# A routed expert block: GpSimd's row writes in twos, its stores in threes, an unrolled store loop, and two steps of VectorE sooner

## The chip, the core and the metric

The kernel runs on one core of one Trainium2 chip. Its time is the device time of that core in microseconds. TensorE, VectorE, ScalarE, GpSimd and SyncE (SP) run their own instruction streams and wait for each other by semaphores. A DMA adds 16 to its semaphore when it has landed. In the profile PE is TensorE's products, PEld its weight loads, DVE is VectorE, ACT is ScalarE, POOL is GpSimd.

## The reference, cut to what matters

```python
def reference(x, ctx, g_xattn, g_ffn, Wq, Wk, Wv, Wo, Wg, bg, W1, b1, W2, b2):   # x, ctx: (8, 512, 256)
    def xattn(x, context):                       # 16 heads of 16; attention is over the heads of a token
        Q, K, V = [(a @ W.T).reshape(b, l, 16, 16).swapaxes(-2, -1)
                   for a, W in ((x, Wq), (context, Wk), (context, Wv))]
        attn = softmax(einsum('blih,bljh->blij', Q, K) / 4)
        return einsum('blij,bljh->blih', attn, V).swapaxes(-2, -1).reshape(b, l, 256) @ Wo.T
    def ffn(x):                                  # 8 experts, one per token, width 256
        idx = argmax(softmax(x @ Wg + bg))
        y = einsum('tei,eih->teh', gelu(einsum('th,ehi->tei', x, W1) + b1), W2) + b2
        return y at idx
    x = x + tanh(g_xattn[0]) * xattn(layernorm(x), ctx)
    return x + tanh(g_ffn[0]) * ffn(layernorm(x))
```

## The kernel before, in words

4096 tokens are 32 tiles of 128 rows, taken as 16 pairs of tiles in the attention part (about 0 to 200 us). Two pairs make a batch (8 batches, 0 to 7). For each batch VectorE picks each token's expert (pick_1 to pick_7; pick_7 makes the one-hot `oh_b`), TensorE counts ranks with it (`ranks`, L535 and L537), VectorE makes row numbers (place_1 to place_3), and GpSimd writes the rows of a tile with one indirect DMA to `routed_rows` in DRAM, sorted by expert (`route_tile`, L1411; four writes per batch). Each write adds 16 to the semaphore `routed`. The row that is written carries the mean and the inverse deviation of its token; GpSimd raises the variance to the power -0.5 in `pow_x1` (L1404 and L1406, "the pow step").

The expert part works on 39 blocks of 128 routed rows. Per block b: SP fetches the rows (`fetch`, L391), VectorE normalises them (`norm_b`, L1111), TensorE transposes (L641), ScalarE copies (L800), TensorE runs layer 1 (L651), ScalarE the GELU (L793), TensorE layer 2 (L670), VectorE adds bias and residual (`finish`, L1128 to L1132), and GpSimd writes the 128 rows to `out_rows` with an indirect DMA (`store`, L1467). ScalarE also copies the block's layer 1 weights (L785). TensorE's slot b is layer1(b), layer2(b-1), transpose_b(b+2). ScalarE's is gelu(b), copy_xbt(b+2), copy_w1(b+3). VectorE's is `ahead(b)`, the normalisation of block b+3, and then `behind(b)`, the finish of block b-1. There are 8 buffers for finished rows, each with a semaphore `stored[j]`, j = b % 8; VectorE's finish of b waits for the store of b-8.

Blocks 0 to 15 may start before the last rows are written. So the part overlaps with the end of attention and with batches 6 and 7, whose picking, ranks and row numbers are spread over the first slots by hand. SP fetches block 16 and on when the table of blocks is made (`tab_done`) and all 32 writes have landed.

For the last three blocks (36, 37, 38) VectorE computes bias and residual ahead in `prepare` (L1146), and `finish_ahead` (L1157) adds only the product, for block 38 in two halves. YL_ORDER lists in what order the three are prepared.

GpSimd's program is in order: the loop over pairs, `end()`, then stores 0 to 15 written out with the last batch's four writes behind store 3, then a loop with 8 stores per turn (blocks 16 to 31), then blocks 32 to 38 written out. In all of them a store with an odd number is followed by a wait for the landing of the store before it, except from block 36 on. In the loop and before block 16 a wait goes through `wait_apart`, which takes a further instruction.

The helpers `wait_apart` and `slots` stay as they are.

## Time and profile before

| | us |
|---|---|
| median of 3 runs | 291.73 (291.23 to 291.84) |
| the profiled execution | 290.77 |
| its span in the profile | 288.9 |
| TensorE's products busy | 275.6 |
| VectorE busy | 211.3 |
| GpSimd busy | 130.4 |
| ScalarE busy | 102.9 |

The span runs from the first to the last instruction; 1.9 us of the profiled execution lie around it. The granted clock of TensorE is full throughout. In a timeline a row gives an instruction's start, its length, and in brackets how long its engine was idle before it and what the profile names as the end of that idle time. An indirect DMA's row shows the time in which GpSimd issues it, not its landing.

### The profile page before, as it was taken

The page shows a single profiled execution, that of the slowest core. Times are in us where ns is not written, and L with a number is a line of the kernel's source. Part 1 is how long each engine was busy: PE and PEld are TensorE (multiplying, and loading weights), DVE is VectorE, ACT ScalarE, POOL GpSimd, SP SyncE. Part 2 cuts the span into 40 slices and gives each one's busy share as a digit, 9 for nine tenths or more (in the row PEclk, how much of TensorE's full clock was granted, in tenths as well). Part 3 has the DMA queues.
Part 4 walks back from the last instruction along what each step waited for, and adds up shares of the span by engine and source line. Part 5 has one row for each costly group of instructions (what it writes and reads, how often), then busy time and mean ns, then how long its engine had stood idle before and what let it go on. Part 6 is the DMA issues. An engine that isn't in the chain of part 4 may idle for free.

```text
span 288.9 us, 9745 instructions
## 1 busy us (share of the span) xinstructions
PE 275.6 (95%) x3185; PEld 219.2 (76%) x3186; DVE 211.3 (73%) x613; ACT 102.9 (36%) x258; POOL 130.4 (45%) x156
## 2 busy tenths in 40 slices
PE   8999999999999999999999999799987999999990
PEld 7667777677776776777767777578976988998980
DVE  7667667787796786878778778788876875765661
ACT  2120311302203113031130321337664776776750
POOL 9623032243524525336254452702754554455565
PEclk9999999999999999999999999999999999999999
DMA  7955355476664755647656634414244344433311
GB/s 233 297 163 161 71 138 146 127 205 171 192 178 144 224 175 182 208 122 225 170 174 226 193 103 135 126 42 117 84 149 133 112 151 143 121 113 124 97 71 40
DMA packets 31242, 43.24 MB, mean 150 GB/s; under 512 B 7662, under 2 KB 18543, under 8 KB 31217
## 3 DMA queue, kind: packets, MB, share of 16 engines
q1 hardware_dynamic: 17760, 21.35, 26.7%
q10 hardware_dynamic: 10048, 12.99, 15.1%
q0 software_dynamic: 3408, 8.59, 8.4%
q8 instruction: 12, 0.20, 0.3%
q14 instruction: 14, 0.11, 0.2%
HBM read 24.83 MB, written 10.60 MB: 123 GB/s over the span
## 4 chain that ended last, share of the span: by engine, by line
PE 75%; issue 7%; POOL 5%; DVE 5%; DMA 5%; ACTq 1%; ACT 1%; POOLq 0%; DVEq 0%
PE ps_qo L439 18%; PE ps_pr L410 18%; PE ps_av L484 11%; PE ps_so L465 9%; POOL out_rows L1467 5%; PE ps_av L670 3%; PE ps_so L651 3%; PE ps_to L670 3%; PE ps_tr L474 3%; PE ps_tr L651 3%; PE ps_to L497 2%; PE ps_pr L641 2%; DMA sb_kb<-sb_y_k 2%; DMA out_rows<-sb_q_n,sb_tok_i 2%; DVE sb_kb L1279 1%
## 5 line engine op out<-in xcount | busy, mean ns | idle before, releaser
L410 PE MATMUL ps_pr<-sb_wkv,sb_ct 128*128 128x512 f32 x120 | 57.7, 605 | 0.0
L718 ACT ACTIVATE sb_pe_x<-sb_pe_x 128x512 f32<-128x512 f32 x16 | 10.1, 631 | 111.9 <-DVE sb_pe_x L894 100.6
L1397 POOL TENSOR_SCALAR sb_ve<-sb_mv 128x2 f32<-128x2 f32 x16 | 3.5, 220 | 78.0 <-DVE sb_mv L853 75.2
L1411 POOL DMA_INDIRECT routed_rows<-sb_xs,sb_pos_i x32 | 32.7, 1023 | 12.5 <-issue 7.4
L410 PEld LDWEIGHTS ps_pr<-sb_wkv,sb_ct 128*128 128x128 f32 x120 | 20.5, 190 | 17.7 <-issue 17.3
L484 PE MATMUL ps_av<-sb_vb,sb_at 128*32 128x128 f32 x1024 | 31.8, 274 | 1.5 <-issue 1.5
L465 PE MATMUL ps_so<-sb_kb,sb_y_q 128*32 128x128 f32 x1024 | 31.2, 273 | 0.5 <-DMA sb_kb<-sb_y_k 0.5
L484 PEld LDWEIGHTS ps_av<-sb_vb,sb_at 128*32 128x32 f32 x1024 | 27.2, 110 | 5.1 <-issue 4.9
L439 PE MATMUL ps_qo<-sb_wog,sb_ot 128*128 128x264 f32 x120 | 29.6, 388 | 0.0
L439 PEld LDWEIGHTS ps_qo<-sb_wog,sb_ot 128*128 128x128 f32 x120 | 22.5, 190 | 9.2 <-issue 6.4
L465 PEld LDWEIGHTS ps_so<-sb_kb,sb_y_q 128*32 128x32 f32 x1024 | 28.0, 110 | 1.9 <-issue 1.5
L439 PE MATMUL ps_qo<-sb_wqg_c,sb_xt 128*128 128x264 f32 x120 | 29.3, 387 | 0.0
L879 DVE STREAM_TRANSPOSE sb_y_q<-sb_q_n 128x512 f32<-128x512 f32 x16 | 17.4, 1090 | 15.6 <-ACT sb_q_n L713 15.5
L785 ACT COPY sb_kb<-sb_w_all 128x514 f32 x39 | 24.2, 622 | 11.0 <-issue 10.4
L303 POOL TENSOR_TENSOR sb_cn<-sb_om,sb_rt 128x512 f32<-128x512 f32 x14 | 18.1, 1290 | 20.3 <-DVE sb_om L918 20.3
L1467 POOL DMA_INDIRECT out_rows<-sb_y_k,sb_tok_i x20 | 20.0, 1001 | 15.8 <-issue 9.8
L439 PEld LDWEIGHTS ps_qo<-sb_wqg_c,sb_xt 128*128 128x128 f32 x120 | 21.7, 190 | 3.8 <-issue 0.5
L670 PE MATMUL ps_av<-sb_w,sb_ht 128*128 x80 | 20.6, 380 | 1.1 <-issue 0.6
L651 PE MATMUL ps_tr<-sb_ct,sb_kb 128*128 128x128 f32 x152 | 20.3, 276 | 1.3 <-ACT sb_ct L800 1.3
L651 PE MATMUL ps_so<-sb_ct,sb_kb 128*128 128x128 f32 x160 | 21.2, 276 | 0.2 <-ACT sb_ct L800 0.2
L670 PE MATMUL ps_to<-sb_w,sb_ht 128*128 x76 | 20.0, 385 | 0.3 <-ACT sb_ht L793 0.2
L651 PEld LDWEIGHTS ps_so<-sb_ct,sb_kb 128*128 128x128 f32 x160 | 19.5, 192 | 0.5 <-ACT sb_ct L800 0.5
(159 smaller groups left out, 493.0 us busy)
## 6 DMA issues: line engine op xcount, KB each, us to landing
sb_x<-x_in ACTq DMA_DIRECT2D x16, 256.0 KB, 3.5
sb_kb<-sb_y_k SPq DMA_DIRECT2D x124, 32.0 KB
sb_vb<-sb_y_v SPq DMA_DIRECT2D x120, 32.0 KB
sb_ct<-ctx_in ACTq DMA_DIRECT2D x14, 256.0 KB, 3.1
sb_xt<-xt_in_ ACTq DMA_DIRECT2D x14, 256.0 KB, 4.6
sb_xb<-routed_rows SPq DMA_DIRECT2D x25, 134.0 KB
sb_w_all<-w_in_ SPq DMA_DIRECT2D x4, 514.0 KB
sb_w<-w_in SPq DMA_DIRECT2D x4, 512.0 KB
```

Of the source, the lines that this page charges most:

```text
L303: eng.tensor_tensor(cn[:].rearrange("p u h i -> p h u i"), om[:].rearrange("p h (u i) -> p h u i", u=2), rt[:].rearrange("p (u i) -> p u i ...
L410: last = pe.matmul(pr[:, s * 512:(s + 1) * 512], lhsT=ct[i][:, kc, s, :], rhs=wkv[:, :, kc, :], start=(kc == 0), stop=(kc == KC - 1))
L439: last = pe.matmul(dst[:, s * 512:s * 512 + DE], lhsT=src[:, kc, s, :], rhs=w[:, kc, :], start=(kc == 0), stop=(kc == KC - 1))
L465: last = pe.matmul(so[32 * q:32 * q + 32, r * P:(r + 1) * P], lhsT=y_q[:, 4 * q + r, u:u + 2, :].rearrange("p a b -> p (a b)"), rhs=kb[i][ ...
L484: last = pe.matmul(av[32 * q:32 * q + 32, r * P:(r + 1) * P], lhsT=at[:, 4 * r + q, u:u + 2, :].rearrange("p a b -> p (a b)"), rhs=vb[i][: ...
L651: last = pe.matmul(h_ps[i][:, ic * P:(ic + 1) * P], lhsT=w1_sb[q % W1_RING][:, kc * D + ic * P:kc * D + (ic + 1) * P], rhs=xbt[i][:, kc, : ...
L670: last = pe.matmul(dst, lhsT=ht[i][:, ic, :], rhs=w2_sb[:, bass.ds(ex, 1), ic, first:end].rearrange("p a d -> p (a d)"), start=(ic == 0), ...
L718: act.activation(pe_x[:], pe_x[:], ACT.Exp, scale=float(H) ** -0.5).then_inc(exp_done, 1)
L785: act.copy(w1_sb[q % W1_RING], w1_all[:, bass.ds(ex, 1), :].rearrange("p a f -> p (a f)")).then_inc(w1_done, 1)
L879: dve.transpose(y_q[:, :, 0:3:2, :].rearrange("p a u i -> p i u a"), q_n[:].rearrange("p s (h i) -> p i s h", h=H)).then_inc(yq_out, 1)
L1411: pool.indirect_dma_start(rows, bass.IndirectOffsetOnAxis(ap=row_numbers(batch)[:, c:c + 1], axis=0), rows_of(j)[:, s, :], None).then_inc( ...
L1467: pool.indirect_dma_start(out, bass.IndirectOffsetOnAxis(ap=tok_i[j][:, 0:1], axis=0), yf[j], None, bounds_check=limit, oob_is_err=False). ...
```

## The change

- Batch 5's four writes in `end()`: the pow step of pair 12 goes between the first two and the last two.
- Batch 6: the pow step of pair 15 goes between its first and second write; a wait for the first write's landing goes ahead of the third, and one for the third's landing behind the fourth.
- The second and fourth write of batches 6 and 7 signal a new semaphore, `routed_odd`, and SP waits for both semaphores before block 16.
- Batch 7, behind store 3: a wait for store 2's landing is put ahead of the writes; the wait behind the second write is for the first write alone, that behind the fourth for the third alone. Before, they were for all so far.
- Stores: from block 4 on they go in threes (4, 5, 6, then 7, 8, 9, and so on). Behind the third GpSimd waits for the landing of the second, up to block 33.
- The loop for blocks 16 to 31 is unrolled; its waits are plain ones.
- VectorE's `pick_7` of the last batch goes ahead of the normalisation of block 7, and `prepare(38)` goes from slot 36 to slot 35.

```diff
-YL_ORDER = (0, 2, 1)
+YL_ORDER = (2, 0, 1)
@@ SP
-            sp.wait_ge(routed, 32 * pairs)
+            sp.wait_ge(routed, 32 * pairs - 64)
+            sp.wait_ge(routed_odd, 64)
@@ VectorE
-                if known and b == blocks - AHEAD:
+                if known and b == blocks - AHEAD - 1:
                     prepare(blocks - 1)
@@
             behind(3, 3, 0)
+            pick_7(m)
             ahead(4, 4, 0)
-            pick_7(m)
@@ GpSimd
-                route_tile(2 * (batch % 2) + i // 2, i % 2, batch)
+                route_tile(2 * (batch % 2) + i // 2, i % 2, batch, routed_odd if i % 2 else routed)
+
+            def late_routed(batch, i):
+
+                return 64 * (last_batch - 1) + 32 * (batch - last_batch + 1) + 16 * (i // 2 + 1)
@@ end()
-                for j in range(2):
-                    route(2 * ((m - 1) % 2) + j, m - 1)
+                route(2 * ((m - 1) % 2), m - 1)
                 pow_x1(n - 2, (n - 2) % 4)
+                route(2 * ((m - 1) % 2) + 1, m - 1)
                 pow_x1(n - 1, (n - 1) % 4)
                 pow_x1(n, n % 4)
-                for i in range(2):
-                    route_nth(m, i)
+                route_nth(m, 0)
                 pow_x1(n + 1, (n + 1) % 4)
-                for i in range(2, 4):
-                    route_nth(m, i)
+                route_nth(m, 1)
+                pool.wait_ge(routed, late_routed(m, 1))
+                route_nth(m, 2)
+                route_nth(m, 3)
+                pool.wait_ge(routed, late_routed(m, 3))
@@ the stores
                 store(b, b % RING, b // RING)
                 if b == 3:
+                    pool.wait_ge(stored[2], 16)
                     for i in range(4):
                         route_nth(last_batch, i)
                         if i % 2 == 1:
-                            pool.wait_ge(routed, 32 * pairs - 16 * (3 - i))
-                elif b % 2 == 1:
+                            pool.wait_ge(routed, late_routed(last_batch, i))
+                elif b == 1 or b > 3 and b % 3 == 0:
                     pool.wait_ge(stored[(b - 1) % OUT], 16 * ((b - 1) // OUT + 1))
-            def store_in_twos(b, q, turn):
-                store(b, q, turn)
-                if isinstance(b, int) and b >= blocks - 3:
-                    return
-                if q % 2 == 1 and isinstance(b, int):
-                    pool.wait_ge(stored[q - 1], 16 * (turn + 1))
-                elif q % 2 == 1:
-                    wait_apart(pool, stored[q - 1], 16 * (turn + 1), passed_pool)
-
-            block_slots(pool, store_in_twos, 0)
+            for b in range(EARLY, blocks):
+                store(b, b % RING, b // RING)
+                if b % 3 == 0 and b < blocks - 3:
+                    pool.wait_ge(stored[(b - 1) % OUT], 16 * ((b - 1) // OUT + 1))
```

Line numbers of the changed kernel are 2 higher in TensorE's and VectorE's part and 8 higher for the store.

GpSimd in `end()`, before: `sb_xs_1` and `sb_xs_0` are the two batches' row buffers, `sb_ve1` the pow step's variance.

```order
L1411 DMA routed_rows<-sb_xs_1,sb_pos_i 33792x268 [waits pos_done]
L1411 DMA routed_rows<-sb_xs_1,sb_pos_i 33792x268
L1411 DMA routed_rows<-sb_xs_1,sb_pos_i 33792x268 [waits pos_done]
L1411 DMA routed_rows<-sb_xs_1,sb_pos_i 33792x268
L1404 TENSOR_SCALAR sb_ve1<-sb_xs_0 128x2 [waits res_pow,res_step]
L1406 TENSOR_TENSOR sb_xs_0<-sb_ve1,sb_neg_half 128x2 [waits res_var]
```

The same place in the changed kernel:

```order
L1413 DMA routed_rows<-sb_xs_1,sb_pos_i 33792x268 [waits pos_done]
L1413 DMA routed_rows<-sb_xs_1,sb_pos_i 33792x268
L1406 TENSOR_SCALAR sb_ve1<-sb_xs_0 128x2 [waits res_pow,res_step]
L1408 TENSOR_TENSOR sb_xs_0<-sb_ve1,sb_neg_half 128x2 [waits res_var]
L1413 DMA routed_rows<-sb_xs_1,sb_pos_i 33792x268 [waits pos_done]
L1413 DMA routed_rows<-sb_xs_1,sb_pos_i 33792x268
```

The pow step now parts the four writes into two pairs.

GpSimd from batch 7's first write on, behind store 3, in the changed kernel; `tok_i_j` is the row list of the store that signals `stored[j]`:

```order
L1475 DMA out_rows<-sb_q_n,sb_tok_i_3 4096x256 [waits yf_done]
L1413 DMA routed_rows<-sb_xs_1,sb_pos_i 33792x268 [waits stored2,pos_done]
L1413 DMA routed_rows<-sb_xs_1,sb_pos_i 33792x268
L1413 DMA routed_rows<-sb_xs_1,sb_pos_i 33792x268 [waits routed]
L1413 DMA routed_rows<-sb_xs_1,sb_pos_i 33792x268
L1475 DMA out_rows<-sb_y_k_1,sb_tok_i_4 4096x256 [waits routed,yf_done]
L1475 DMA out_rows<-sb_y_k_1,sb_tok_i_5 4096x256 [waits yf_done]
L1475 DMA out_rows<-sb_y_v_0,sb_tok_i_6 4096x256 [waits yf_done]
L1475 DMA out_rows<-sb_y_v_0,sb_tok_i_7 4096x256 [waits stored5,yf_done]
```

Before, the first write has no wait for `stored2`, and the wait for `stored4` stands ahead of store 6; here store 6 follows store 5 at once, and store 7 waits for `stored5`.

VectorE around the last batch's one-hot, before: `sb_ct` is the normalised block, `sb_lw` the picked expert's code.

```order
L976 TENSOR_REDUCE sb_lw<-sb_le 128x4 [waits pick_step]
L1128 ISA [waits y_done]
L1128 TENSOR_TENSOR sb_yo<-ps_av,sb_b 128x256
L1130 TENSOR_TENSOR sb_tok_i<-sb_xb,sb_skip 128x1
L1132 SCALAR_TENSOR_TENSOR sb_q_n<-sb_yo,sb_tg,sb_xb 128x256 [waits yb_done]
L1111 TENSOR_SCALAR sb_ct<-sb_wkv 128x256 [waits xbt_done,xb_in7]
L982 TENSOR_TENSOR sb_oh_b<-sb_le,sb_lw 128x32 [waits rank_done,pick_step]
```

And in the changed kernel:

```order
L1134 SCALAR_TENSOR_TENSOR sb_q_n<-sb_yo,sb_tg,sb_xb 128x256 [waits yb_done]
L984 TENSOR_TENSOR sb_oh_b<-sb_le,sb_lw 128x32 [waits rank_done,pick_step]
L1113 TENSOR_SCALAR sb_ct<-sb_wkv 128x256 [waits xbt_done,xb_in7]
L1130 ISA [waits y_done]
L1130 TENSOR_TENSOR sb_yo<-ps_to,sb_b 128x256
```

The one-hot changes places with the normalisation of block 7.

## Rows read from the trace of the kernel before

**Rows 1.** The page: busy us, share and instructions; shares of the chain.

```profile
PE 275.6 (95%) x3185; PEld 219.2 (76%) x3186; DVE 211.3 (73%) x613; ACT 102.9 (36%) x258; POOL 130.4 (45%) x156
PE 75%; issue 7%; POOL 5%; DVE 5%; DMA 5%; ACTq 1%; ACT 1%; POOLq 0%; DVEq 0%
```

**Rows 2.** Table by stretch: us, busy us per engine, granted clock, DMA share, GB/s.

```profile
222.00:282.00 60.00, 59.66 (x415) 54.20 (x414) 39.84 (x130) 42.22 (x116) 31.72 (x32) 1.00 0.39 119
```

**Rows 3.** Timeline at batch 5's writes: start, us, instruction, idle time before and releaser.

```profile
181.40 1.09 POOL L1411 DMA_INDIRECT routed_rows<-sb_xs,sb_pos_i  x1 [0.17 <-issue]
...
186.31 0.32 POOL L1404 TENSOR_SCALAR sb_ve<-sb_xs 128x2 f32<-128x2 f32 x1
...
187.54 1.04 PE L484 MATMUL ps_av<-sb_vb,sb_at 128*32 128x128 f32 x28 [1.15 <-issue]
...
188.80 0.72 DVE L918 STREAM_TRANSPOSE sb_om<-ps_av 128x512 f32<-128x512 f32 x1 [1.97 <-PE ps_av L484]
```

**Rows 4.** Timeline at the last batch's one-hot and ranks, 206 to 213 us.

```profile
206.44 0.19 DVE L953 TENSOR_TENSOR sb_lg<-sb_xs 128x32 f32<-128x32 f32 x1 [0.92 <-POOL sb_xs L1406]
...
210.29 0.18 PE L535 MATMUL ps_qo<-sb_oh_b,sb_tri 128*128 128x40 bf16 x1 [0.36 <-DVE sb_oh_b L982]
...
210.54 0.99 POOL L1467 DMA_INDIRECT out_rows<-sb_y_k,sb_tok_i  x1 [0.30 <-issue]
...
210.91 0.37 ACT L800 COPY sb_ct<-ps_pr 128x256 f32<-128x256 f32 x1 [2.09 <-remote]
...
211.17 1.13 PE L670 MATMUL ps_av<-sb_w,sb_ht 128*128 x4 [0.61 <-issue]
...
212.55 0.63 ACT L793 ACTIVATE sb_ht<-ps_tr,sb_kb 128x128 f32<-128x128 f32 x2
```

**Rows 5.** Timeline at the run of stores 2, 3 and batch 7's writes.

```profile
217.57 0.96 POOL L1411 DMA_INDIRECT routed_rows<-sb_xs,sb_pos_i  x1 [0.30 <-issue]
...
219.54 0.37 ACT L800 COPY sb_ct<-ps_pr 128x256 f32<-128x256 f32 x1 [2.97 <-PE ps_pr L641]
...
219.96 1.16 PE L651 MATMUL ps_tr<-sb_ct,sb_kb 128*128 128x128 f32 x8 [1.34 <-ACT sb_ct L800]
...
221.54 1.13 PE L670 MATMUL ps_av<-sb_w,sb_ht 128*128 x4 [0.42 <-ACT sb_ht L793]
```

**Rows 6.** Timeline: block 4 finished, stores 4 and 32, layer 1 starts of four blocks.

```profile
214.34 0.48 DVE L1132 SCALAR_TENSOR_TENSOR sb_y_k<-sb_yo,sb_tg,sb_xb 128x256 f32<-128x256 f32 x1
...
225.05 0.99 POOL L1467 DMA_INDIRECT out_rows<-sb_y_k,sb_tok_i  x1 [2.41 <-DVE sb_y_k L1132]
...
226.68 1.06 PE L651 MATMUL ps_so<-sb_ct,sb_kb 128*128 128x128 f32 x8
...
257.31 1.06 PE L651 MATMUL ps_tr<-sb_ct,sb_kb 128*128 128x128 f32 x8
...
259.29 1.06 PE L651 MATMUL ps_so<-sb_ct,sb_kb 128*128 128x128 f32 x8
...
278.33 0.98 POOL L1467 DMA_INDIRECT out_rows<-sb_y_k,sb_tok_i  x1 [1.08 <-issue]
...
279.42 1.05 PE L651 MATMUL ps_so<-sb_ct,sb_kb 128*128 128x128 f32 x8
```

**Rows 7.** Timeline of the tail, 280 us to the end.

```profile
280.51 0.48 DVE L1157 SCALAR_TENSOR_TENSOR sb_y_k<-ps_av,sb_tg,sb_yo 128x256 f32<-128x256 f32 x1
...
281.02 0.98 POOL L1467 DMA_INDIRECT out_rows<-sb_q_n,sb_tok_i  x1 [0.42 <-DMA out_rows<-sb_y_k,sb_tok_i]
...
281.82 0.61 PE L670 MATMUL ps_tr<-sb_w,sb_ht 128*128 x4
...
283.49 0.48 DVE L1157 SCALAR_TENSOR_TENSOR sb_y_k<-ps_to,sb_tg,sb_yo 128x256 f32<-128x256 f32 x1 [1.93 <-issue]
...
285.62 0.35 DVE L1157 SCALAR_TENSOR_TENSOR sb_y_v<-ps_tr,sb_tg,sb_y_q 128x128 f32<-128x128 f32 x1 [1.03 <-remote]
...
286.27 0.98 POOL L1467 DMA_INDIRECT out_rows<-sb_y_v,sb_tok_i  x1 [0.31 <-issue]
```

More of the change, by code:

```diff
@@ L251, in flamingo_block @@
         routed = sem("routed")
+        routed_odd = sem("routed_odd")
         pad_in = sem("pad_in")
@@ L1406, in pow_x1, with route_tile @@
                 pool.tensor_tensor(rows_of(j)[:, :, RSTD], ve1[:], neg_half[:], ALU.pow).then_inc(res_pow, 1)
-            def route_tile(j, s, batch):
+            def route_tile(j, s, batch, done):
                 c = 2 * (j % 2) + s
                 pool.indirect_dma_start(rows, bass.IndirectOffsetOnAxis(ap=row_numbers(batch)[:, c:c + 1], axis=0),
-                                        rows_of(j)[:, s, :], None).then_inc(routed, 16)
+                                        rows_of(j)[:, s, :], None).then_inc(done, 16)
             def route(j, batch):
@@ L1417, in route @@
                 for s in range(2):
-                    route_tile(j, s, batch)
+                    route_tile(j, s, batch, routed)
             def route_nth(batch, i):
```

## The prediction

> **What bounds the kernel now.** I read the busy line and the shares of the chain first, then the stretch of the expert blocks, then each engine's timeline where the change sits. TensorE is busy for 275.6 of 288.9 us and holds 75% of the chain; GpSimd holds 5% [rows 1]. TensorE's last product, of block 38, is over at 281.82 + 0.61 = 282.43 us [rows 7]. So TensorE bounds the kernel up to there, and the stores do after it. Gaps of TensorE stand in few places: 1.15 us at 187.54 [rows 3], 0.36 and 0.61 at 210.29 and 211.17 [rows 4], 1.34 and 0.42 at 219.96 and 221.54 [rows 5]. From 222 to 282 it is busy for 59.66 of 60 us [rows 2].
>
> The tail: VectorE adds the bias of block 37 at 283.49 and of the last half of block 38 at 285.62, 3.2 us after the product; the last store starts at 286.27 [rows 7]. GpSimd is behind all the way to there. It stores block 4 at 225.05, though its rows were finished at 214.34 + 0.48 = 214.82, and block 32 at 278.33 [rows 6]: 28 blocks in 53.28 us, 1.90 each or 3.81 a pair. TensorE needs (279.42 - 226.68) / 26 = 2.03 us a block [rows 6], so GpSimd catches up by 0.13 us a block, too little for its ten.
>
> The gaps: where GpSimd issues indirect DMAs back to back (0.96 to 1.0 us each, 0.30 between), the end of TensorE's work reaches the other engines late. In the run of four that ends at 217.57 + 0.96 = 218.53, ScalarE's copy at 219.54 had stood 2.97 us for a transpose, and TensorE then stood 1.76 us in two pieces [rows 5]. In the run that ends at 210.54 + 0.99 = 211.53, ScalarE's copy stood 2.09 us and its next GELU began at 212.55 [rows 4]. I call this the **hold**; both times it is over 1.0 us behind the last issue. Pairs with a wait between them hardly show it: an undisturbed slot is 259.29 - 257.31 = 1.98 us [rows 6], so the 26 slots lost 26 x 0.05 = 1.3 us, 0.1 per pair. A run of four cost 1.76.
>
> **The change part by part.** The profiled execution took 290.77 us (span 288.9 and 1.9 around it); the median of the runs is 291.73. I make the sum against the former; it moves the median by as much.
>
> (a) Batch 5's writes, behind the loop's exit. Now four stand in a row from 181.40 to 186.3, and TensorE stands 1.15 us in the middle of one group of products [rows 3]. The pow step goes between the second and the third. Its operands are there: now it starts at 186.31 with no idle time [rows 3]. It takes about 1.1 us, so the second pair is over at 187.4, and nobody waits for its writes before the fetches. VectorE's transpose of those products, at 188.80, carries the chain on. If the gap goes wholly it gains 1.15; if it has another cause, 0. With a hold of 0.6 to 1.0 behind 187.4 the transpose starts 0.4 to 0.8 sooner. I take **-0.6**.
>
> (b) Batch 6's writes and the one-hot. The pow step moves ahead of the second write and ends about a microsecond sooner, so VectorE's 0.92 us of waiting for it at 206.44 goes [rows 4]. The one-hot then also goes ahead of a normalisation (0.4 us). It is ready at about 208.8, not 210.1, and TensorE's 0.36 for it and 0.61 behind it [rows 4] are covered by layer 1 of block 5. The writes now form a run of three, over at about 209.1, instead of a run of two writes and two stores over at 211.53, so ScalarE's copy comes at about 209.7. What is late next is ScalarE's GELU, still 1.64 us behind that copy. Bounds: -0.3 (the one-hot gains alone and the hold stays) and -1.3 (VectorE's whole gain). I take **-0.9**, near the two gaps of 0.97 that go.
>
> (c) Stores 2, 3 and the last batch's writes. Now stores 2, 3 and writes 0, 1 are the run of 1.76 us. Afterwards the wait for store 2's landing parts the stores from the writes. But between the writes the wait is now for the first of two: for both it was 2.41 us ahead of store 4 [rows 6], for the first of a pair it is 0.42 where the loop is unrolled [rows 7]. A run of four is made again, of the four writes. I take **0**; bounds -1.76 (0.4 us is enough of a break) and +0.3. Behind the new waits stand the stores, 10 us late anyway, and SP's fetch of block 16 onward, which asks for all writes. The shorter waits give back what the added one takes, so the fetch stays hidden, as it is now [rows 2].
>
> (d) Stores in threes. Up to block 15 a run takes 3.81 + 1.28 = 5.09 us, 1.70 a block. From 16 on, unrolled, a pair takes 281.02 - 278.33 = 2.69 [rows 6, 7], as the last ones do now, and three take 3.97. GpSimd starts block 4 some 2 us sooner and TensorE's blocks come 1.5 us sooner: it is 9.7 us behind. It gains 6.1 + stalls - 5.1, some 1.9 us per three, up to block 15, and 3 per three after: level with VectorE at about block 19. From there each store waits for its own block, they stand 2 us apart, and no run is left. The price is four runs of three, back to back, beside working TensorE. No such run is in the trace. Its bounds are 0.1 (a pair) and 1.76 (four); I take the middle, 0.93, since a three has one issue more than the one and one less than the other: 4 x 0.93 = **+3.7**. The pairs' **-1.3** goes. Bounds of both together: -0.9 and +7.5 (five runs at 1.76).
>
> (e) Tail. The bias step of block 38 moves to a place where VectorE waits for TensorE's product anyway. With GpSimd level, block 36 is done at 280.51 + 0.48 and stored at 281.3, 37 at 282.6, 38 at 283.9, against 286.27 [rows 7]: **-2.4**. If the moved step lets 36 come 0.6 sooner, -3.0; if VectorE's last steps stay late, -0.3.
>
> Sum: -0.6 - 0.9 + 0 + 3.7 - 1.3 - 2.4 = **-1.5**: 289.3 profiled, **290.2 us** as a median.
>
> **The rivals.** *A: threes cost no more than twos.* For: pairs cost next to nothing, and TensorE's ends pass in the first half of a run. Against: the stands of 2.09 and 2.97 us. Then (d) is 4 x 0.1 - 1.3 = -0.9, and the time is 291.73 - 0.6 - 0.9 - 0.9 - 2.4 = 286.9 us. The Trainium skill (DMA: Bandwidth & Descriptors, Anatomy of one DMA) says that many descriptors can be emitted before their cost shows; by that sentence this rival is right, while the trace shows a cost on other engines, at 219.54 and 219.96 [rows 5].
>
> *B, slower: a run of three costs what four cost.* The place is blocks 4 to 18, the price 1.76 for each of five runs, 8.8 - 1.3 = +7.5, and the time 291.73 - 0.6 - 0.9 + 7.5 - 2.4 = 295.3 us. The change is slower from where a run costs more than (0.6 + 0.9 + 1.3 + 2.4) / 4 = 1.3 us. For: the hold lasts 1.0 us beyond the last issue, so a three's is 1.28 us longer than a pair's, and a slot of 1.98 us has room for only a part of that. Against: only a product that ends early in the hold pays in full.
>
> *C: the change doesn't do what it says.* GpSimd's runs move, but the last three stores are issued back to back as now and VectorE's last steps stay late: (e) is -0.3; and (a) is 0, since the gap at 187 is no hold. 291.73 - 0.9 + 2.4 - 0.3 = 292.9 us.
>
> **How the numbers follow.** Forecast 0.42, its own range 288.6 to 291.9 (a three at 0.6 to 1.3); A 0.28; B 0.16; C 0.14. Within 0.2% is about what a measurement of this kernel can tell from no change: 291.15 to 292.31. Of the forecast 0.33 lies below 291.15; with A that makes faster 0.61. Within: 0.07 of the forecast, 0.05 of C, 0.02 of B, 0.14 in all. Slower: 0.25. The range goes down to A's 286.9, less half a microsecond for (c), 286.4, and up to 293.4, which leaves out the dearer part of B.
>
> **What the profile of the changed kernel would show.** (a) A pow step between two pairs of writes, and no gap of TensorE inside L484's group. (b) The rank product without idle time before it, and no wait of VectorE for GpSimd's pow. (c) Stores 2 and 3 apart from the writes, the four writes close together, and ScalarE's copy standing near them. (d) Three stores 1.28 us apart up to about block 15, from 19 on one each 2 us; some 3.5 us of gaps in TensorE's blocks, all before block 18. (e) The last store's start 1.5 us behind TensorE's end instead of 3.8. It is wrong if TensorE shows no gaps beside the threes (A), if more than 1.3 us stand beside each (B), or if the last store starts over 3 us behind TensorE's end (C).

## The result, and the profile of the changed kernel

The changed kernel is slower. Its median is 294.12 us (291.48 to 297.82, 22 executions) against 291.75 (290.61 to 293.58, 22 executions) for the kernel before, run beside it; the ratio is 1.006, 95% interval 1.0037 to 1.0083. The forecast was 290.2 with a range of 286.4 to 293.4: the time is above the range. (The medians here take every execution; the ratios leave out those more than 1.5% above the fastest of the same kernel, five of the changed kernel's 22, so they show less than the medians where the times spread.) The executions of the changed kernel also lie further apart (6.3 us from end to end, against 3.0), and the one that was profiled is the lowest of them, 291.48 (span 289.6; before 290.77 and 288.9). So the first reading below shows a mild case. A second profile, near the median, stands with the experiments.

The page of the changed kernel, busy time and chain, answers to [rows 1]. TensorE is busy for 3.1 us more than before and holds 91% of the chain; GpSimd, which held 5%, is off it:

```profile
PE 278.7 (96%) x3185; PEld 221.6 (77%) x3186; DVE 210.3 (73%) x613; ACT 103.3 (36%) x258; POOL 129.4 (45%) x156
PE 91%; DVE 3%; issue 2%; ACT 1%; ACTq 1%; POOL 0%; DVEq 0%
```

More busy time for the same products means a lower clock or stretched groups. The table by stretch (us, TensorE's busy time, that of its weight loads, VectorE's, ScalarE's and GpSimd's, then the granted clock, DMA share, GB/s) shows where. [Rows 2] had 59.66 of 60 us at 1.00:

```profile
220.00:230.00 10.00, 8.21 (x44) 7.07 (x43) 5.32 (x21) 4.82 (x14) 5.80 (x7) 0.83 0.36 111
230.00:285.00 55.00, 52.61 (x364) 47.55 (x362) 33.95 (x107) 37.34 (x101) 28.78 (x30) 1.00 0.38 116
```

A mean of 0.83 over 10 us, of two levels (2.4 and 1.2 GHz), is 3.4 us at the lower one, in which 1.7 us of work is lost, since TensorE was busy throughout it. TensorE's timeline has the places (start, us, instruction, in brackets the idle time before and what ended it):

```profile
187.73 0.38 PE L486 MATMUL ps_av<-sb_vb,sb_at 128*32 128x128 f32 x3 [0.32 <-issue]
188.47 0.53 PE L486 MATMUL ps_av<-sb_vb,sb_at 128*32 128x128 f32 x10 [0.36 <-issue]
...
211.13 1.13 PE L672 MATMUL ps_av<-sb_w,sb_ht 128*128 x4 [0.74 <-ACT sb_ht L795]
...
223.67 1.16 PE L653 MATMUL ps_tr<-sb_ct,sb_kb 128*128 128x128 f32 x8 [1.30 <-issue]
225.32 1.76 PE L672 MATMUL ps_av<-sb_w,sb_ht 128*128 x4 [0.49 <-ACT sb_ht L795]
...
235.96 1.13 PE L672 MATMUL ps_av<-sb_w,sb_ht 128*128 x4 [0.49 <-issue]
...
240.65 1.13 PE L672 MATMUL ps_av<-sb_w,sb_ht 128*128 x4 [0.42 <-issue]
...
285.08 0.71 PE L672 MATMUL ps_av<-sb_w,sb_ht 128*128 x4 [1.32 <-ACT sb_ht L795]
285.62 0.61 PE L672 MATMUL ps_tr<-sb_w,sb_ht 128*128 x4
```

Against [rows 3 to 5]: the gap of 1.15 us at 187.54 is down to two small pieces, and the 0.36 for the ranks is gone. The gap of 1.34 and 0.42 is there still, now 1.30 and 0.49, and behind its second piece the same four products take 1.76 us instead of 1.13: the clock had fallen. Two gaps of 0.4 to 0.5 us and one of 1.32 at block 38 are new. TensorE ends at 286.23, 3.8 us later than in [rows 7]. GpSimd's timeline and ScalarE's copy beside it:

```profile
218.11 0.99 POOL L1413 DMA_INDIRECT routed_rows<-sb_xs,sb_pos_i  x1 [1.00 <-issue]
219.40 0.96 POOL L1413 DMA_INDIRECT routed_rows<-sb_xs,sb_pos_i  x1 [0.30 <-issue]
221.00 0.95 POOL L1413 DMA_INDIRECT routed_rows<-sb_xs,sb_pos_i  x1 [0.64 <-DMA routed_rows<-sb_xs,sb_pos_i]
222.26 0.96 POOL L1413 DMA_INDIRECT routed_rows<-sb_xs,sb_pos_i  x1 [0.30 <-issue]
223.24 0.37 ACT L802 COPY sb_ct<-ps_pr 128x256 f32<-128x256 f32 x1 [2.86 <-PE ps_pr L643]
224.46 0.99 POOL L1475 DMA_INDIRECT out_rows<-sb_y_k,sb_tok_i  x1 [1.25 <-issue]
...
286.90 0.98 POOL L1475 DMA_INDIRECT out_rows<-sb_y_v,sb_tok_i  x1 [0.71 <-DVE sb_y_v L1159]
```

The four writes of the last batch are the new run: ScalarE's copy stands 2.86 us beside it, as it stood 2.97 in [rows 5]. The last store starts 0.67 us behind TensorE's end instead of 3.84. So the end was mended more than forecast, and TensorE lost more than that before it.

### The profile page after: what moved, and what is told of

It is laid out like the page before. It is cut to its first block, busy times and chain, and to the rows that moved or that the text cites. A ratio compares the mean times of both kernels' runs of the same rounds, so it can differ in the third digit from the quotient of the medians.

```text
span 289.6 us, 9704 instructions
## 1 busy us (share of the span) xinstructions
PE 278.7 (96%) x3185; PEld 221.6 (77%) x3186; DVE 210.3 (73%) x613; ACT 103.3 (36%) x258; POOL 129.4 (45%) x156
## 4 chain that ended last, share of the span: by engine, by line
PE 91%; DVE 3%; issue 2%; ACT 1%; ACTq 1%; POOL 0%; DVEq 0%
PE ps_pr L412 19%; PE ps_qo L441 18%; PE ps_av L486 10%; PE ps_so L467 8%; PE ps_so L653 7%; PE ps_av L672 7%; PE ps_tr L653 5%; PE ps_to L672 5%; PE ps_pr L643 4%; PE ps_tr L476 3%; PE ps_to L499 2%; PE ps_av L580 1%; PE ps_pr L426 1%; PE ps_to L433 1%; ACTq L785 1%
## 5 line engine op out<-in xcount | busy, mean ns | idle before, releaser
L672 PE MATMUL ps_av<-sb_w,sb_ht 128*128 x80 | 21.5, 392 | 3.7 <-ACT sb_ht L795 2.7
L653 PE MATMUL ps_so<-sb_ct,sb_kb 128*128 128x128 f32 x160 | 22.1, 283 | 0.2 <-ACT sb_ct L802 0.2
L653 PEld LDWEIGHTS ps_so<-sb_ct,sb_kb 128*128 128x128 f32 x160 | 20.4, 199 | 0.5 <-ACT sb_ct L802 0.5
L653 PEld LDWEIGHTS ps_tr<-sb_ct,sb_kb 128*128 128x128 f32 x152 | 18.5, 191 | 1.8 <-issue 1.5
```

Of the source, the lines that this page charges most:

```text
L653: last = pe.matmul(h_ps[i][:, ic * P:(ic + 1) * P], lhsT=w1_sb[q % W1_RING][:, kc * D + ic * P:kc * D + (ic + 1) * P], rhs=xbt[i][:, kc, : ...
L672: last = pe.matmul(dst, lhsT=ht[i][:, ic, :], rhs=w2_sb[:, bass.ds(ex, 1), ic, first:end].rearrange("p a d -> p (a d)"), start=(ic == 0), ...
```

## The experiments

Kernels that are told of together ran on one chip, against executions of the kernel before among them. "Before" is its median there. I call GpSimd's standing time between two groups of issues its **pause**.

| run | median | before | ratio of the times, 95% |
|---|---|---|---|
| changed kernel, stores in twos (e1) | 295.37 | 292.35 | 1.0093, 1.0059 to 1.0126 |
| before, threes, unrolled (e2) | 294.68 | 292.35 | 1.0078, 1.0051 to 1.0105 |
| before, twos, unrolled (e3) | 296.23 | 292.35 | 1.0117, 1.008 to 1.0154 |
| before, writes and one-hot (e4) | 291.59 | 292.35 | 0.9979, 0.9952 to 1.0006 |
| changed kernel again (a1) | 293.39 | 291.53 | 1.0012, 0.9971 to 1.0053 |
| e3 again (a2) | 294.81 | 291.53 | 1.0094, 1.0055 to 1.0133 |
| e3, idle pow from block 16 (g5) | 292.63 | 291.53 | 1.0018, 0.9981 to 1.0055 |
| e1, idle pow from block 16 (g6) | 292.66 | 291.53 | 1.0024, 0.9985 to 1.0064 |
| changed kernel, idle pow (h1) | 292.76 | 292.34 | 1.0022, 0.9994 to 1.005 |
| before, singles, two idle additions (h2) | 295.53 | 292.34 | 1.013, 1.0085 to 1.0174 |
| e3, half the rows (h5) | 292.83 | 292.34 | 1.0012, 0.9985 to 1.0039 |
| changed kernel, store loop of before (e6) | 291.91 | 292.34 | 0.9985, 0.9954 to 1.0016 |
| e4 and one idle pow (k1) | 291.84 | 292.16 | 0.9985, 0.9955 to 1.0016 |
| e4 again (k2) | 291.53 | 292.16 | 0.9998, 0.9962 to 1.0035 |

Four more runs (g1 to g4) fell on a chip that behaves otherwise; they stand further below.

### Is it the threes, the writes or the unrolled loop?

e1 puts the twos back into the changed kernel, e2 and e3 change the store loop of the kernel before alone, e4 keeps the writes and the one-hot alone.

```diff
 e1: changed kernel, and the same before block 16    e3: kernel before, loop unrolled, this condition
-                if b % 3 == 0 and b < blocks - 3:
+                if b % 2 == 1 and b < blocks - 3:
 e2: kernel before, the changed kernel's unrolled loop of threes
 e4: changed kernel without it
-            for b in range(EARLY, blocks):
-                ...
+            block_slots(pool, store_in_twos, 0)            (and twos before block 16)
-YL_ORDER = (2, 0, 1)         (and prepare(blocks - 1) back behind block 36)
+YL_ORDER = (0, 2, 1)
```

> The changed kernel with its stores in twos again from block 4 on (loop unrolled; the writes, one-hot and tail edits kept). Theory T, the threes cost (about 0.9 us each beside working TensorE, one of them with a drop of the granted clock to half behind it): the time falls from 294.1 by 3.5 or more, to 288.5 to 290.5 us, and no gap over 0.6 us stands in TensorE's blocks from 222 to 245. Theory W, the four writes of the last batch, parted only by short waits, cost and start it: the time stays at 293.5 to 294.5 and a gap of 1 us or more still stands near 222. Theory U, the unrolled loop costs (GpSimd's stores move onto other work): 293 or more, with gaps that are spread over the blocks.

> The kernel before with its stores in threes and unrolled, nothing else changed. Theory T: slower than before by 2 to 4 us less the gain at the end of 1 to 2 us: 293 to 295 us. Theory W (the writes cost, the threes don't): 290 to 291.5 us. Theory U: 293 to 295 us as well, and the kernel with unrolled twos tells it from T.

> The kernel before with the store loop unrolled and still in twos, nothing else changed. Theory T: GpSimd catches up by 1.1 us a pair from block 16 on, the last store starts 1.5 us behind TensorE's end instead of 3.8: 289.0 to 290.5 us. Theory U: 292.5 us or more. Theory W says the same as T here.

> The kernel before with the edits of the writes and the sooner one-hot alone (batch 5 and 6 split by the pow steps, the waits for the first of two, stores 2 and 3 parted from the last batch's writes); stores in twos in the loop and the tail as before. Theory T: the prediction's terms for them, -1.5 us: 290.2 (289.5 to 291.5). Theory W: the last batch's four writes in a row cost 1.8 us or more and set the clock back: 292.5 to 294 us, with a gap of TensorE of over 1 us near 222.

Theory T, mine, isn't enough. Without any three the changed kernel is no faster (295.37), and the kernel before with nothing but its loop unrolled is 3.9 us slower: the worst of the four. In threes the unrolled loop costs 2.3. The writes and the one-hot alone do no harm (-0.8, the interval just holds zero), so W falls. What e3 shows is U: something that unrolling brings, with a place, behind block 16. But e1 doesn't refute T. It took the threes out and got another thing for them: its profile's large gaps stand beside the pairs of blocks 16 to 20, 1.34 us an issue,

```profile
250.18 1.16 PE L653 MATMUL ps_tr<-sb_ct,sb_kb 128*128 128x128 f32 x8 [1.92 <-issue]
...
254.96 2.07 PE L672 MATMUL ps_av<-sb_w,sb_ht 128*128 x4 [3.62 <-ACT sb_ht L795]
```

where the changed kernel, whose GpSimd is level with VectorE from store 17 or 18 on, has none. In the repeated run of unrolled twos (a2) TensorE's timeline reads

```profile
250.35 1.16 PE L651 MATMUL ps_tr<-sb_ct,sb_kb 128*128 128x128 f32 x8 [0.77 <-issue]
...
255.75 2.07 PE L670 MATMUL ps_av<-sb_w,sb_ht 128*128 x4 [4.24 <-ACT sb_ht L793]
```

and the table by stretch, of TensorE alone,

```profile
250.00:260.00 10.00, 5.41 (x24) 0.66 0.20 58
```

Some 5 us of standing still in the middle of the blocks, and then half clock (2.07 us for products that take 1.13). GpSimd and ScalarE beside it:

```profile
246.19 1.17 POOL L1467 DMA_INDIRECT out_rows<-sb_y_v,sb_tok_i  x1 [0.30 <-issue]
247.70 0.98 POOL L1467 DMA_INDIRECT out_rows<-sb_y_k,sb_tok_i  x1 [0.34 <-issue]
...
250.38 0.98 POOL L1467 DMA_INDIRECT out_rows<-sb_q_n,sb_tok_i  x1 [0.42 <-DMA out_rows<-sb_y_k,sb_tok_i]
251.67 0.98 POOL L1467 DMA_INDIRECT out_rows<-sb_q_n,sb_tok_i  x1 [0.30 <-issue]
253.13 0.98 POOL L1467 DMA_INDIRECT out_rows<-sb_y_k,sb_tok_i  x1 [0.48 <-DMA out_rows<-sb_q_n,sb_tok_i]
...
254.98 0.62 ACT L793 ACTIVATE sb_ht<-ps_so,sb_kb 128x128 f32<-128x128 f32 x2 [3.64 <-remote]
```

From 244.87 to 254.11 GpSimd issues seven stores with pauses of 0.34 to 0.48 us. ScalarE's GELU starts at 254.98, 0.87 us behind the last of them, though the products that it needs, of the block before, were over at 248.51. The bracket names no instruction, only an event that came late. This is the hold of the prediction, in a run of pairs that I had taken to be parted. In the five profiles with the loop its pauses are 0.95 us or more; unrolled they are 0.34 to 0.48 here. The loop as such need not be the reason: the pairs before block 16 are written out in both kernels, and their pauses are 0.89 us or more too. There, as in the loop, the store's wait for its rows goes through `wait_apart`; from block 16 of the unrolled code, and in the last stores of [rows 7], it is a plain one. No run parts the two.

### Does a pause end it?

g5 and g6 put one small pow of GpSimd on an idle tile behind each wait from block 16 on; a1 and a2 are the changed kernel and e3 once more, on the same chip.

```diff
                 if b % 2 == 1 and b < blocks - 3:
                     pool.wait_ge(stored[(b - 1) % OUT], 16 * ((b - 1) // OUT + 1))
+                    pool.tensor_tensor(idle[:], ve[:], neg_half[:], ALU.pow).then_inc(idled, 1)
```

> The changed kernel once more, beside the others on one chip. The last four runs showed no gap of TensorE beside runs of four and six of GpSimd's issues, nor the gap inside the products at 187 us, in code that was as in the kernel before there; the hold may be a thing of the chip that a run falls on. Theory C (it is): where the kernel before shows its gaps at 187 and 220 us on this chip, this one is 1.5 to 2.5 us slower than before (293.5 to 295); where the hold is absent, it is 2 us or more faster than before. Theory P alone (only pauses decide, on every chip): 1.5 to 2.5 us slower on any chip.

> The kernel before with the store loop unrolled and in twos, once more. Theory C: with the hold on this chip 3 to 4 us slower than before, with gaps of 3 us and more in sum between 245 and 262; without it 1 to 2 us faster than before and no gap there. Theory P alone: 3 to 4 us slower on any chip.

> As the run before this one, with GpSimd's idle pow (0.9 us with what lies around it) behind each wait from block 16 on. Theory P, on a chip that shows the hold: its pairs now stand 1.3 us apart instead of 0.42 and the gaps between 245 and 262 us are gone: 3 us or more faster than the unrolled twos without the pow, 290.5 to 292.5. If pauses don't matter but the run's length in issues over a longer stretch does: gaps of 1 us and more remain, and it is within 1.5 us of the unrolled twos.

> The changed kernel with its stores in twos, unrolled, and the idle pow behind each wait from block 16 on; writes, one-hot and tail edits kept. Theory P, on a chip that shows the hold: 289 to 291.5 us, faster than the changed kernel by 2 us or more and than the kernel before by 0.5 or more, with the gaps near 223 (1.4 us in sum) as the only ones over 0.5 after 215. The rival: TensorE has gaps of a microsecond and more beside the pairs after 245, and it is no faster than the changed kernel.

With the pow the 5 us at 250 are gone. g5's only gap of TensorE from 223 to its end, and GpSimd there:

```profile
248.57 1.13 PE L672 MATMUL ps_av<-sb_w,sb_ht 128*128 x4 [0.38 <-ACT sb_ht L795]
...
249.61 0.72 POOL L1466 TENSOR_TENSOR sb_idle<-sb_ve,sb_neg_half 128x2 f32<-128x2 f32 x1 [0.23 <-DMA out_rows<-sb_y_k,sb_tok_i]
250.52 1.04 POOL L1475 DMA_INDIRECT out_rows<-sb_q_n,sb_tok_i  x1 [0.19 <-POOL sb_idle L1466]
```

So work that does nothing gave 2.2 us back (292.63 against 294.81; by the ratios, whose intervals only just touch, the same). The pause is the cause, or what it stands for. g6 wasn't faster than the kernel before, though I had expected that: with the pow a pair takes 3.5 to 4.3 us, GpSimd doesn't catch up, and its last store starts at 286.52, as late as in [rows 7].

a1 is the case near the median (293.37 in its profile). TensorE, and VectorE at the first gap:

```profile
231.21 0.53 DVE L1113 TENSOR_SCALAR sb_ct<-sb_xb 128x256 f32<-128x256 f32 x1 [3.96 <-DMA sb_xb<-routed_rows]
231.79 0.44 PE L643 MATMUL ps_pr<-sb_cst,sb_ct 128*128 128x128 f32 x2 [1.68 <-issue]
...
239.73 1.12 PE L672 MATMUL ps_to<-sb_w,sb_ht 128*128 x4 [0.39 <-issue]
241.71 1.16 PE L653 MATMUL ps_tr<-sb_ct,sb_kb 128*128 128x128 f32 x8 [0.64 <-issue]
246.42 2.07 PE L672 MATMUL ps_av<-sb_w,sb_ht 128*128 x4 [3.55 <-ACT sb_ht L795]
```

Two things come together. The first gap isn't a hold: VectorE stands for the fetch of a block's rows. The last batch's writes now wait for store 2's landing (1.40 us here) and for the first write's (1.34), the last of them starts at 223.98, and SP asks for block 16 at 229.55, against 227.89 in the kernel before. In e6, further below, the same fetch starts at 231.02 and TensorE stands for 1.99 us. The others are the hold: GpSimd issued four threes (blocks 4 to 15) from 226.02 to 243.45, with pauses of 0.99, 1.15 and 0.99 us, and a further store 0.80 later; the 3.55 and the half clock stand behind the last of them:

```profile
246.00:250.00 4.00, 3.58 (x13) 0.57 0.30 82
```

These are threes before the unrolled part, so in the changed kernel itself it is a chain of threes that costs. In the mild execution the same threes had pauses of 1.39, 1.14 and 1.45. So a few tenths of a microsecond of landing time seem to decide whether a delay adds up and whether a fetch comes late, and that would spread the changed kernel's times; it is argued from two profiles. By the median a1 is 1.9 us slower than before, while its ratio, 1.0012, can't be told from 1.

### The pause, the rate, the threes, or the rows?

h1 is the changed kernel with the pow behind all its waits; h2 has no wait for a landing, but two idle additions behind each single store; h5 is e3 with the stores of the first 64 rows.

```diff
 h1: changed kernel
                 if b % 3 == 0 and b < blocks - 3:
                     pool.wait_ge(stored[(b - 1) % OUT], 16 * ((b - 1) // OUT + 1))
+                    rest()
 h2: kernel before, unrolled (rest is two additions here)
-                if b % 2 == 1 and b < blocks - 3:
-                    pool.wait_ge(stored[(b - 1) % OUT], 16 * ((b - 1) // OUT + 1))
+                if b < blocks - 3:
+                    rest()
 h5: kernel before, unrolled
-                ... IndirectOffsetOnAxis(ap=tok_i[j][:, 0:1], axis=0), yf[j], ...
+                ... IndirectOffsetOnAxis(ap=tok_i[j][0:P // 2, 0:1], axis=0), yf[j][0:P // 2], ...
```

> The changed kernel with GpSimd's idle pow (0.9 us) behind each of its waits between the threes, so that a three is followed by a pause of about 2 us instead of 1.0 and goes at some 1.8 us a block instead of 1.5. The prediction's term (each run of three costs 0.9 us by itself): four gaps of TensorE of about 0.9 us remain, and more threes, so it is slower than the changed kernel or equal. Theory R (what costs is the mean rate of issues over several runs: below some 1.6 us an issue the delay adds up from run to run): no gap over 0.4 us between 226 and 280 us, no half clock there, and 1.5 us or more faster than the changed kernel, unless VectorE comes to wait for stores.

> The kernel before, its store loop unrolled, no wait for a landing at all behind a store; instead two small idle additions of GpSimd (0.22 us each) behind each store, so that single stores stand about 0.75 us apart, 1.75 a block. Theory P (only a pause of about a microsecond lets the delay go): the delay adds up from store to store as in the unrolled twos, gaps of 3 us and more in sum, 294 us or more. Theory R (the mean rate decides): no gap over 0.4 us after 226, 290 to 292 us, and the last store less than 3 us behind TensorE's end.

> The unrolled twos with stores of the first 64 rows of a block only (the other rows of the output aren't written). If the delay comes with each row's descriptor of an indirect DMA: with half of them the gaps that the unrolled twos show between 245 and 262 (3 to 5 us and the half clock) go, 290 to 292 us. If it comes with each issue, whatever its size, or with GpSimd's being level: gaps as in the unrolled twos, 294 or more.

h1 has five threes; the wait in front of the pow grew shorter by as much as the pow took, so the pauses are 0.97 to 1.94 us and not the 2 that I had meant. TensorE, and GpSimd at the last of the gaps:

```profile
237.09 1.13 PE L674 MATMUL ps_to<-sb_w,sb_ht 128*128 x4 [1.16 <-DVE sb_yo L1132]
...
241.90 1.13 PE L674 MATMUL ps_to<-sb_w,sb_ht 128*128 x4 [0.60 <-ACT sb_ht L797]
...
246.84 1.13 PE L674 MATMUL ps_to<-sb_w,sb_ht 128*128 x4 [0.73 <-ACT sb_ht L797]
...
251.42 1.13 PE L674 MATMUL ps_to<-sb_w,sb_ht 128*128 x4 [0.37 <-ACT sb_ht L797]
...
251.68 1.04 POOL L1483 DMA_INDIRECT out_rows<-sb_q_n,sb_tok_i  x1 [0.19 <-issue]
253.03 0.99 POOL L1483 DMA_INDIRECT out_rows<-sb_y_k,sb_tok_i  x1 [0.30 <-issue]
...
255.32 1.13 PE L674 MATMUL ps_av<-sb_w,sb_ht 128*128 x4 [1.66 <-ACT sb_ht L797]
```

The first three (blocks 4 to 6) has no gap behind it, the other four have 1.16, 0.60, 0.73 and 0.37: (0 + 1.16 + 0.60 + 0.73 + 0.37) / 5 = 0.57 on average. The 1.66 stands behind two issues only, stores 19 and 20, 0.97 us after a three: not the price of a three, but what had added up by then. The 1.16 and the 0.37 belong to threes behind pauses of 1.94 and 1.75 us. Theory R, which said no gap over 0.4, is wrong on this: a three that stands alone can cost, somewhat less than the prediction's 0.93. But none grows to 3 us and the clock stays at 1.00. By the median h1 is 0.4 us from its kernel before, where a1 was 1.9; by the ratios (1.0022 and 1.0012) the two are alike, so that the pow made this kernel faster isn't shown.

h2 has single stores with 0.72 us between them, mostly 1.74 from start to start, from 251 on:

```profile
271.65 1.02 POOL L1476 DMA_INDIRECT out_rows<-sb_q_n,sb_tok_i  x1 [0.15 <-issue]
273.39 1.02 POOL L1476 DMA_INDIRECT out_rows<-sb_y_k,sb_tok_i  x1 [0.15 <-issue]
...
280.73 0.71 PE L672 MATMUL ps_av<-sb_w,sb_ht 128*128 x4 [1.88 <-DVE sb_y_k L1159]
```

and TensorE's table by stretch has

```profile
222.00:278.00 56.00, 55.53 (x392) 1.00 0.39 116
```

There is no gap but one of 0.49 at 222.47. Theory P (only a pause of a microsecond helps) is wrong: 0.72 will do, behind each store. The time is bad all the same, 295.53: until 250 the idle steps and their waits took 2.1 us a block, GpSimd fell behind TensorE, VectorE stood for a store's landing (the 1.88 at 280.73) and the last store began 8 us behind TensorE's end. I had forecast 290 to 292 there and missed that.

h5 halves the rows of each issue. An issue takes 0.91 us instead of 0.98, and the gaps at 250 are gone, but so is the cause as stated: from 228 on the landings left pauses of 0.95 to 1.02 us, and GpSimd was level by 246. In that stretch of pairs, 3.2 us each, TensorE still has

```profile
232.43 1.13 PE L670 MATMUL ps_av<-sb_w,sb_ht 128*128 x4 [0.32 <-ACT sb_ht L793]
...
235.17 1.13 PE L670 MATMUL ps_to<-sb_w,sb_ht 128*128 x4 [0.50 <-issue]
...
238.29 1.12 PE L670 MATMUL ps_av<-sb_w,sb_ht 128*128 x4 [0.77 <-issue]
```

Small gaps that grow, at half the rows. And at 218.22, behind two such stores and two whole writes in a row, TensorE stood 2.35 us, against 1.34 + 0.42 in [rows 5]. This speaks for the issue and against the rows as what counts, but it doesn't settle it.

Taken together, by the mean distance of issues over several of them: 1.90 us (loop of before) and 1.79 (h2 from 251.87 on): no gap. 1.63 to 1.8 (g5, 237 to 250): one of 0.38. 1.6 (h5): 0.32, 0.50, 0.77. 1.53 to 1.79, in threes (h1): 0.4 to 1.7. 1.56 to 1.67, in threes (the changed kernel's mild profile): 0.42 and 0.49. 1.51 to 1.57, in threes (a1): up to 3.55. 1.35 (e1, e3, a2): 1.9 to 4.2. An estimate from these rows: each issue holds something for some 1.6 us, though GpSimd can issue every 1.28, and the difference adds up until GpSimd stands. It fits the rows of this section; what the something is, no run shows, nor whether it lies in the issuing or in the landings that go with it.

### A chip without the hold

g1 to g4 ran together, before theory C was there.

```diff
 g1: e3 and the pow behind every wait          g3: changed kernel, twos, the pow behind every wait,
 g2: e3, wait for the pair's second landing        the last batch's pairs wait for both landings
 g4: g2 without the waits after 13, 19, 27 and 29, with one after 14 (runs of three, four and six)
-                    pool.wait_ge(stored[(b - 1) % OUT], 16 * ((b - 1) // OUT + 1))
+                    pool.wait_ge(stored[b % OUT], 16 * (b // OUT + 1))
```

> The kernel before with its store loop unrolled and in twos, as in the run with unrolled twos, but GpSimd does one small idle pow (0.72 us by the rows of before) after each wait, so that it stands about 1.1 us between two issues of a pair's end and the next pair instead of 0.42. Theory P (new): the hold isn't set by how many issues stand in a row, but by a pause of GpSimd of a microsecond or more; pauses of 0.3 to 0.66 us don't end it, and the stretch from 245 to 260 us, where the unrolled twos show gaps of TensorE of 0.99, 2.56 and 1.83 us, shows none over 0.2: 289.5 to 291.5 us. Theory L, what costs is that GpSimd catches up with VectorE (the catching-up is nearly as fast here, 1.65 us a block): gaps of over 1 us in TensorE's blocks and 294 us or more.

> The kernel before, unrolled, in twos, each pair followed by a wait for its second store's landing instead of its first's: GpSimd stands some 1.7 us between the pairs and hardly catches up (3.97 us for two blocks). Theory P: no gap of TensorE over 0.2 us after 225; TensorE ends as in the kernel before, and the last store is up to 2 us later than there: 291 to 294 us. Theory U (the unrolled code itself costs, by its instruction fetches or otherwise): gaps of 1 us and more between 245 and 262 and a time of 295 us or more.

> The changed kernel with two differences: the last batch's two pairs of writes each wait for both landings, and the stores go in twos with the idle pow behind each wait (pause 1.1 us). Theory P: the gaps of 1.30 and 0.49 (or 0.69 and 0.74) near 223 shrink to under 0.5 in sum, the half clock doesn't come, the blocks from 225 to 280 have no gap, the last store starts less than 2.5 us behind TensorE's end: 287.5 to 290 us, faster than the kernel before. Theory L: 293 us or more.

> The pairs with waits for the second landing, but with a run of three stores at blocks 12 to 14, of four at 18 to 21 and of six at 26 to 31, each followed by a pause of about 1.7 us. It measures the gap of TensorE beside a run by its length. Theory P: three 0.3 to 0.8 us, four about 1.8 us, six 3.5 us or more; TensorE's gap grows by about the 1.28 us of each further issue. Theory of the prediction (a slot of 1.98 us takes up a part, each run pays once): three 0.9, four 1.8, six 2.5 us.

Medians: 292.60, 303.23, 295.77 and 299.98 us beside 290.61 for the kernel before (286.55 to 294.68). They can't test what they were made for. None shows the gaps at 187 and 220 us of [rows 3, 5], though g1, g2 and g4 have the same code there, and g4's runs of four and six leave no mark on TensorE (table by stretch around them):

```profile
259.00:268.00 9.00, 9.00 (x65) 1.00 0.43 123
273.00:282.00 9.00, 8.32 (x57) 1.00 0.19 69
```

The 0.68 us that the second row lacks are the start of a wait for VectorE, which stood 1.91 us for a store's landing. So here the hold is absent, and its lack isn't bought by pauses. The chip is the likely reason, but only these four kernels ran there, once. One gap of [rows 4] is there all the same: 0.61 us at the ranks in g1 and g4, 0.77 in g2. That one is no hold. What these kernels cost is another thing: with waits for second landings GpSimd falls eight blocks behind, and VectorE stands for the buffer of the block eight before. In g4:

```profile
239.43 0.42 DVE L1128 TENSOR_TENSOR sb_yo<-ps_av,sb_b 128x256 f32<-128x256 f32 x1 [3.44 <-DMA out_rows<-sb_y_k,sb_tok_i]
```

I had put up to 2 us on that wait and it cost 12.6 in g2. Theory C was half right: on the other chips that I saw the hold was there. Whether the changed kernel is faster than before on a chip like this one wasn't measured.

### The end, and the writes again

e6 is the changed kernel with the store loop of before; k1 puts one pow behind the wait after block 33 of e4; k2 is e4 again.

```diff
 k1:
                 if q % 2 == 1 and isinstance(b, int):
                     pool.wait_ge(stored[q - 1], 16 * (turn + 1))
+                    if b == blocks - 6:
+                        pool.tensor_tensor(idle[:], ve[:], neg_half[:], ALU.pow).then_inc(idled, 1)
```

> The changed kernel with only the stores as before (loop, twos): the writes, the one-hot and the bias step of block 38 remain. The difference to the run with the writes and the one-hot alone is the bias step. Theory: that step by itself gives 0 to 0.5 us, since the last stores stay in a row; 290.8 to 291.7 us beside a kernel before at 291.5 to 292.3, and it is the fastest version of all. If the bias step costs (its wait is moved ahead of VectorE's work for block 35): 292 or more.

> The writes and the one-hot alone (stores and tail as before), and one idle pow of GpSimd behind the wait after block 33. In the two profiles with these writes TensorE stood 2.5 to 2.7 us for the GELU of block 38, beside stores with pauses of 0.43 to 0.63. Theory R: with 1.3 us of pause there the GELU comes over a microsecond sooner and that gap is under 1.5 us; the stores' own end moves little, so 0.2 to 0.8 us faster than the writes alone, 290.9 to 291.5 beside a kernel before at 292.0. The rival: the end is set by GpSimd's stores, each of which comes 0.9 us later: slower by 0.5 to 0.9 us.

> The writes and the one-hot alone, a second time, to narrow the interval. The first time gave 0.9979 of the time before, from 0.9952 to 1.0006. If the gain of (a) and (b) of the prediction is real, though smaller than the 1.5 us forecast: 0.4 to 1.0 us faster than before. If it was chance: within 0.3 us of it.

e6 has the whole change but its stores, and its median is 0.4 us below that of before: what makes the change slower is in the stores. The bias step gives nothing that can be told (e6 -0.4 of its before, e4 -0.8, k2 -0.6). The GELU of block 38 is a matter of luck: TensorE stood for it in e4 and in e6,

```profile
282.34 1.22 PE L672 MATMUL ps_av<-sb_w,sb_ht 128*128 x4 [2.70 <-ACT sb_ht L795]
```

```profile
286.36 0.71 PE L672 MATMUL ps_av<-sb_w,sb_ht 128*128 x4 [2.54 <-issue]
```

but neither in k1 nor in k2, so k1 doesn't show that its pow helps. For the writes and the one-hot, twice the median was 0.6 to 0.8 us below that of before, twice the interval holds 1, and the second ratio is 0.9998. It has the lowest medians beside before, but a gain isn't shown.

## Why the prediction was wrong, point by point

Sign and size were wrong. By its steps, from the mild profile where not said otherwise:

- **What bounds the kernel**, TensorE to its end and then the stores, was right; so was the hold as the thing to price.
- **(a) -0.6: right in sign, over-sized.** TensorE's pieces in that group are 0.32 + 0.36 = 0.68 us against 0.34 + 1.15 before, a gain of 0.81. But over nine profiles with the new order the pieces sum to 0.68 to 1.6 us, on average 1.11, and over seven with the old to 1.11 to 1.56, on average 1.41: 0.3, half of what I took.
- **(b) -0.9: a gain, over-sized.** VectorE's wait for the pow and TensorE's 0.36 are gone, but 0.74 stands where 0.61 did: 0.2 us on TensorE. The 0.61 wasn't the hold's to give back, since g1, g2 and g4 have it without any hold. With (a) the runs e4 and k2 give 0.6 to 0.8 by the medians and 0.6 and 0.1 by the ratios, not 1.5.
- **(c) 0: right in sum, wrong in its parts.** In the mild profile the gap stayed (1.30 + 0.49 against 1.76). Over all profiles on chips with the hold it goes by the pause between the writes: with 0.42 to 0.71 us it is 0.94 to 1.79 (seven profiles), with 1.34 and 1.48 (a1 and e6) there is none. But in those two the fetch came late, by 1.68 and 1.99 us of TensorE, so "so the fetch stays hidden" failed: the shorter wait doesn't give back what the added one takes when landings are slow. I also priced every gap by its length alone. Behind the mild profile's gap the clock went to half and took 1.7 us of work, where a gap of the same length had left it at full speed before. That isn't the change's doing: with the old order of the writes it fell there too in e2, g5 and h5, three of seven profiles. The row in e2:

```profile
222.34 1.93 PE L670 MATMUL ps_av<-sb_w,sb_ht 128*128 x4 [0.42 <-issue]
```

- **(d) is the step that failed.** It priced each three by itself, 4 x 0.93 = 3.7, as if the delay of one were over when the next began, and it had no term for the clock. In a1, with pauses of 0.99 to 1.15 us, the delay added up: 0.39 + 0.64 + 3.55 = 4.58 us of gaps and 1.7 us of half clock, 6.3 where I had 3.7 (and took 1.3 off for the pairs). With pauses up to 1.45, in the mild profile, the gaps are 0.91; parted further, in h1, a three costs 0.57 on average. The step also costed the unrolled waits at nothing: "From 16 on, unrolled, a pair takes 281.02 - 278.33 = 2.69". I read that pairs hardly cost from pairs 0.9 us apart and more, and carried it to pairs 0.4 us apart. e3 measures those waits alone: +3.9 us. In the changed kernel GpSimd is level before they matter (forecast: block 19), so by a1's rows its own loss is the threes'. No run isolates that: a kernel with threes up to block 15 and the old loop wasn't tried. e2, the stores of the change alone, is 2.3 slower, where this step had +2.4 and (e) took 2.4 off again. "I take the middle" was a price for one run; none of the bounds was for a chain of them.
- **(e) -2.4: the end itself went further, by 3.2.** The last store starts 0.67 us behind TensorE's end. But now the stores around it, 0.50 us apart from 279.92 on, hold up block 38's GELU for 1.32 us, which the step had not asked for. And in a1 TensorE's end at 287.73 leaves 288.79 for the last store: a short tail behind a late end.
- **The rivals.** A (a three costs nothing) is refuted by h1. The Trainium skill (DMA: Bandwidth & Descriptors, Anatomy of one DMA) says that many descriptors can be emitted before their cost shows; the rows agree for GpSimd's own time, 0.98 us an issue throughout and 0.91 with half the rows, and say nothing of the sort for the engines beside it. B (slower, 295.3) had the sign and nearly the time, by five runs at 1.76; what happened is fewer and larger stalls, so that its time was near is luck. C didn't happen.

In the mild profile the sum closes so: -0.8 (a) - 0.2 (b) + 0.0 (c) + 1.7 (clock) + 0.9 (two gaps at the threes) + 1.3 (block 38) - 3.2 (e) = -0.3, and 0.65 us by which GpSimd's first write stood later (182.05 against 181.40) before anything of the change acts: +0.35 of the span's +0.7. The other 0.35 I can't place. The median is 2.6 us above that profile; a1, 1.9 above it, has 6.26 us in its four gaps after 220, where the mild one has 4.02 in five. a1's own sum is -0.6 (a) - 0.3 (b) - 1.8 (no gap at 220) + 1.7 (the fetch) + 4.6 (the threes) + 1.7 (clock) - 2.8 (e) + 0.3 (first write later, 181.71) = +2.8, against 2.6 by the profiled times.

## What to carry to other kernels

A wait that costs an engine nothing may be what paces it: before a loop is unrolled, a wait shortened or issues put in larger groups, look at how dense the DMA issues become, and price the chain of them, not the single run. A gap of TensorE has a second price, the clock behind it, which a gap of the same length may or may not pay; put it into the range. And where a change makes the executions spread, profile one near the median before the parts are added up.
